# Output projection of a delta-rule attention layer: its first chunks in another order, and o by A of chunks 1 to 3 on VectorE

## What is computed

```
q, k, v = silu(dconv_causal(x @ Wq)), ...        a = sigmoid(x @ Wa + ba)   beta = sigmoid(x @ Wb + bb)
o  = delta_rule(q, k, v, a, beta)                # a scan over 512 tokens, 4 batches, 16 heads of 128 x 128
o  = (o - mean) * rsqrt(var + 1e-5) * ln_w + ln_b    # over the 128 values of each head
o  = o * sigmoid(x @ Wg)
x1 = layernorm(x + o @ Wo)                       # Wo is 2048 x 512
y  = layernorm(x1 + down(silu(x1 @ up) * (x1 @ gate)))   # ternary weights
```

## Time and profile before

| | |
|---|---|
| median of 3 runs | 2786.04 us (2780.75 to 2790.62) |
| the profiled execution | 2770.43 us, its span 2768.7 us |
| TensorE busy in the span | 2549.2 us (92%) |
| VectorE, ScalarE, GpSimd busy | 2039.8, 1164.5, 1439.3 us |
| `attention_out` in the span | about 2013 to 2325 us |

### The profile page before, as it was taken

The page is one execution under the profiler, slowest core; times in us unless marked ns, Lnnn a source line. Parts: engine busy times, 40 slices in busy tenths (PEclk is TensorE's granted clock), DMA queues, the critical chain, the costliest instruction groups (busy, mean ns, idle before and its releaser), DMA issues. The chain is left out here.

```text
span 2768.7 us, 50121 instructions
## 1 busy us (share of the span) xinstructions
PE 2549.2 (92%) x17682; PEld 2205.4 (80%) x17682; DVE 2039.8 (74%) x5887; ACT 1164.5 (42%) x2265; POOL 1439.3 (52%) x1216
## 2 busy tenths in 40 slices
PE   8999999999999589999999999999748897899999
PEld 6888888888888478888898888988637776788887
DVE  4777777677768369999999999999669895333333
ACT  4545444544454222332223322223568784433333
POOL 2644553455346489899998999988322220000000
PEclk9999999999999779999999999999769999999999
DMA  5466546654664765555556656655655544000000
GB/s 134 130 176 172 164 133 176 176 161 135 172 178 140 221 235 213 199 218 200 201 204 236 231 213 234 234 219 199 242 205 197 197 167 153 38 11 11 11 11 15
DMA packets 417317, 454.35 MB, mean 164 GB/s; under 512 B 122496, under 2 KB 367232, under 8 KB 393856
## 3 DMA queue, kind: packets, MB, share of 16 engines
q1 hardware_dynamic: 417152, 452.22, 48.8%
HBM read 321.49 MB, written 131.14 MB: 163 GB/s over the span
## 5 line engine op out<-in xcount | busy, mean ns | idle before, releaser
L355 PE MATMUL pa_ps<-pa_x_hi,pa_w_hi 128*128 128x512 f32 x1296 | 507.8, 392 | 8.2 <-DVE pa_w_lo L394 4.2
L355 PE MATMUL pa_ps<-pa_x_lo,pa_w_hi 128*128 128x512 f32 x1296 | 505.6, 390 | 0.0
L355 PE MATMUL pa_ps<-pa_x_hi,pa_w_lo 128*128 128x512 f32 x1296 | 505.5, 390 | 0.0
L438 DVE SCALAR_TENSOR_TENSOR pa_cv<-pa_y,pa_taps,pa_cv 128x2048 f32<-128x2048 f32 x144 | 359.1, 2494 | 17.8
L1188 DVE TENSOR_TENSOR pb_tmp<-pb_gb,pb_ps 128x112 f32<-128x112 f32 (+6 forms) x1792 | 327.8, 221 | 22.4 <-POOL pb_gb L786 18.1
L1193 DVE TENSOR_TENSOR pb_ps<-pb_ps,pb_tmp 128x112 f32<-128x112 f32 (+6 forms) x1792 | 330.3, 226 | 0.0
L786 POOL TENSOR_TENSOR pb_gb<-pb_gb,pb_ng 128x448 f32<-128x448 f32 (+6 forms) x448 | 319.4, 759 | 7.8 <-DMA pb_gb<-scratch_pairs 4.1
L355 PEld LDWEIGHTS pa_ps<-pa_x_hi,pa_w_hi 128*128 128x128 f32 x1296 | 243.9, 188 | 65.7 <-ACT pa_y L298 8.2
L770 POOL TENSOR_TENSOR all_res<-all_res,pb_crow 128x1024 f32<-128x1024 f32 x120 | 282.4, 2365 | 18.3 <-DMA pb_crow<-scratch_crow 18.3
L355 PEld LDWEIGHTS pa_ps<-pa_x_hi,pa_w_lo 128*128 128x128 f32 x1296 | 244.1, 188 | 51.0
L355 PEld LDWEIGHTS pa_ps<-pa_x_lo,pa_w_hi 128*128 128x128 f32 x1296 | 244.1, 188 | 50.2
(11 more groups left out here) (190 smaller groups left out, 5397.7 us busy)
## 6 DMA issues: line engine op xcount, KB each, us to landing
pb_crow<-scratch_crow SPq DMA_DIRECT2D x30, 2048.0 KB, 10.1
pb_gb<-scratch_pairs SPq DMA_DIRECT2D x64, 896.0 KB, 8.3
pa_o_ng<-scratch_beta SPq DMA_DIRECT2D x16, 1024.0 KB, 7.9
scratch_ng<-pa_o_ng SPq DMA_DIRECT2D x16, 1024.0 KB, 4.5
scratch_A<-pa_o_A SPq DMA_DIRECT2D x16, 1024.0 KB, 4.5
scratch_vt<-pa_o_vt SPq DMA_DIRECT2D x16, 1024.0 KB, 4.5
scratch_q<-pa_o_q SPq DMA_DIRECT2D x16, 1024.0 KB, 6.9
scratch_g<-pa_o_g SPq DMA_DIRECT2D x16, 1024.0 KB, 8.0
```

Source lines behind the costliest of these rows:

```text
L355: last = nc.tensor.matmul(out, w[:, mat, k, :], xx[:, k, b * S:(b + 1) * S], start=(k == 0 and n == 0), stop=(k == KT - 1 and n == 2))
L438: nc.vector.scalar_tensor_tensor(out=out, in0=yy[:, :, k:k + S], scalar=tap(k), in1=out, op0=ALU.mult, op1=ALU.add).then_inc(s_tap, 1)
```

## The change

In the head of `attention_out`:

- o by A of chunks 1, 2 and 3 leaves GpSimd's stream and stands in VectorE's. GpSimd's stream of products begins with chunk 4.
- TensorE does chunk 1's `to_tokens` between blocks 0, 1 and blocks 2, 3 of chunk 0's `to_channels`.
- VectorE sums chunk 1 right behind its half of chunk 0's normalisation; the last eight weight remainders come in one piece behind it; chunk 0's gates are in two halves with chunk 1's normalisation between them.
- ScalarE rounds nine weights first instead of eight, evacuates chunk 0's blocks 2 and 3 only behind chunk 1's squares, and does chunk 1's normalisation before chunk 0's `high`. The squares write into `nrm`, from which chunk 0's blocks are transposed, so there is a new wait for the fourth block.

The regular loops of all engines and SyncE's stream stay as they are. `affine`, `to_channels` and `gate` get an argument `blocks=range(4)`, which is their loop over j.

```diff
 # GpSimd
-            scaled(1, 0, 1)
-            scaled(2, 1, 0)
-            scaled(3, 1, 1)
             with pool.Fori(0, NCH // 2 - 2) as i:
 # ScalarE
-            round_weights(0, 8)
+            round_weights(0, 9)
             squares(0)
             normal(0)
-            round_weights(8, 12)
-            affine(0, 0, True)
+            round_weights(9, 12)
+            affine(0, 0, True, range(0, 2))
             round_weights(12, NH)
+            act.wait_ge(s_b, 4)
+            squares(1)
+            affine(0, 0, True, range(2, 4))
+            normal(1)
             high(0, 0)
-            squares(1)
-            normal(1)
             affine(1, 1, True)
 # TensorE
             to_tokens(0, 0, True)
-            to_channels(0, True)
+            to_channels(0, True, range(0, 2))
             to_tokens(1, 1)
+            to_channels(0, True, range(2, 4))
             pe.wait_ge(s_wo, NH)
 # VectorE
+            def scaled(i, p):
+                dve.wait_ge(s_o[p], 16 * i + 16 * p)
+                dve.wait_ge(s_a[p], 16 * i + 16 * p)
+                nc.vector.tensor_tensor(o_in[p][:, :, :], o_in[p][:, :, :], a_in[p][:, :, :], ALU.mult).then_inc(s_oa, 1)
+
             means(0)
             rest_of_weights(0, 8)
+            scaled(0, 1)
             normal(0, True)
-            rest_of_weights(8, 12)
-            gate(0, 0, 0)
-            rest_of_weights(12, NH)
             means(1)
+            rest_of_weights(8, NH)
+            scaled(1, 0)
+            gate(0, 0, 0, range(0, 2))
+            normal(1)
+            gate(0, 0, 0, range(2, 4))
+            means(2)
             low(0, 0)
-            normal(1)
-            means(2)
+            scaled(1, 1)
             gate(1, 0, 1)
             normal(2)
```

More of the change, by code:

```diff
@@ L1423, in squares, with affine @@
                 nc.scalar.activation(dev[:, :], ssq[:, :], ACT.Sqrt, bias=eps[:, 0:1], scale=1.0 / DV).then_inc(s_dev, 1)
-            def affine(c, p, first=False):
+            def affine(c, p, first=False, blocks=range(4)):
                 if first:
@@ L1429, in affine @@
                     act.wait_ge(s_lo, c - 1)
-                for j in range(4):
+                for j in blocks:
                     act.wait_ge(s_b, 4 * c + j + 1)
@@ L1488, in to_tokens, with to_channels @@
                     last.then_inc(s_t, 1)
-            def to_channels(c, first=False):
-                for j in range(4):
+            def to_channels(c, first=False, blocks=range(4)):
+                for j in blocks:
                     pe.wait_ge(s_na if j < 2 else s_nv, 2 * c + j % 2 + 1)
@@ L1541, in normal, with gate @@
                     last.then_inc(s_nv, 1)
-            def gate(c, i, p):
+            def gate(c, i, p, blocks=range(4)):
                 dve.wait_ge(s_g[p], 16 * i + 16)
-                for j in range(4):
+                for j in blocks:
                     dve.wait_ge(s_ev, 4 * c + j + 1)
```

## The result

The changed kernel took 2767.33 us in the median of 8 runs (2755.23 to 2786.41), the kernel before, run beside it, 2784.86 (2779.88 to 2790.62). The ratio is 0.9934, 95% interval 0.9911 to 0.9956: 18.4 us faster, with 12.3 to 24.8 inside the interval. I had forecast 2775.9 us and 10.1 us of gain, with a range of 2769 to 2784.

What follows compares the result with a forecast made beforehand. The output projection was taken as bound by TensorE's loop behind a late head of ScalarE and VectorE; the first product moves from 2063.2 to 2053.1, a gain of 10.1 us, ratio 0.9964 of 2786.04, so 2775.9 us, range 2769 to 2784.

Steps and rivals of the forecast that it cites:

- What bounds: only the first product's start can be won: Output projection: TensorE paces the loop at 16.7 us a period, so only an earlier first product gains time.
- Start of chunk 0: Head: chunk 1's multiplication takes 2.28 us on VectorE, just hidden; chunk 0's reciprocal starts 1.64 us earlier.
- Chunk 1 between the halves: Head: chunk 1's transposes follow chunk 0's first two blocks; its scalings end at 2035.0 us, before 2048.77.
- the end of 11.8: Head: with chunk 1's 16 transposes at full clock, 1.91 instead of 3.62 us, the gain is up to 11.8 us.
- VectorE is now what ends last: Head: VectorE's remainders, multiplication and gates set the pace; chunk 2's transposes start at 2045.6 us, 11.3 us earlier.
- To the product: Head, chunk 2's transposes to first product: longer than the former 6.28 us; product starts at 2053.1, give or take 0.4.
- The gain: First product starts 10.1 us earlier, kept to the end; sign of being right: 9.5 to 11.5 us earlier.
- How the numbers follow: Whole execution: profiled 2770.43 less 10.1 gives ratio 0.9964; times median 2786.04 gives 2775.9 us, plus range.
- the slow multiplication: Rival, head: multiplication as slow on VectorE as on GpSimd, 4.94 us; gain 5.0, 2781.0 us; chance 0.14.
- the stalls that stay: Rival, head: VectorE's remainders stay slow with GpSimd silent, 1.15 us each; gain 1.6, 2784.4 us; chance 0.02.
- The gain isn't given back: Denies the rival that a late block of chunk 2 or 3 cuts the gain to 0 to 5 us; chance 0.09.
- the loop isn't slower: Denies the rival that GpSimd's multiplication stalls VectorE every loop period: 2.5 us in each of 14, 2811 us; chance 0.05.

Runs made afterwards that it cites:

- the fillers: 8 transposes of the identity matrix ahead of each product's wait, added to the changed kernel; first product to stage end 259.7 to 260.1 us instead of 262.2.
- the two early remainders: Changed kernel with weight remainders 8 and 9 moved ahead of chunk 1's sums on VectorE; head 37.97 us, one execution 2762.4 us.
- before again: The kernel before, unchanged, run against itself: ratio 1.0003, median of 12 runs 2785.4 us.
- loop filled: Changed kernel with 8 transposes of the identity matrix ahead of each product's wait for the og remainder; one execution, 2789.6 us.

## Why the prediction was off

1. *What bounds: only the first product's start can be won.* Right for this change: the loop's periods are the same instructions. But "nothing but" was too strong. The periods aren't all 16.7 us: two to four in each profile take 1.6 us more (two in the profile before), I read only two starts, and the fillers won some 2 us there.
2. *Start of chunk 0.* Right: the multiplication takes 2.28 us and is hidden with 0.38 us to spare, where I had 0.2. Reciprocal 13.03 us behind the stage's first load, as laid out (25.94 - 12.91).
3. *Chunk 1 between the halves.* Mis-sized: I had 22.1 us from the first load to the end of chunk 1's scalings (2035.0 - 2012.91), it took 21.5 (2043.76 - 2022.30), since the clock rose among the transposes. That is the better clock which I had priced as the end of 11.8, for a part of the 16 transposes.
4. *VectorE is now what ends last.* Right, and shown by the two early remainders. Chunk 2's transposes came 31.7 us behind the first load against my 32.7: 0.6 us from step 3, 0.3 from adding up single durations where instructions overlap (eight remainders 4.90 from which the next one starts after 4.81, not 4.96).
5. *To the product.* I had 7.5 us, it took 7.49.
6. *The gain.* 11.1 us in the head in the first pair of profiles, inside my window of 9.5 to 11.5, and 11.6 by the means of both pairs, just outside it; forecast 10.1. The two profiles of the kernel before differ by 0.76 us themselves.
7. *How the numbers follow: "The median of the runs is 2786.04", "with the ratio, 2775.9 us", and a range by "the spread of the runs, which reaches 5.3 below and 4.6 above their median".* This is the step that failed: the terms for the level and for the spread were mis-sized. The three runs, and the five more of the result, happened to lie between 2780 and 2791; 105 lie between 2766.1 and 2804.8 with the median 2780.6, so the level was 5.4 us too high and the spread is 14.5 down and 24.2 up, not 5.3 and 4.6. The profiled execution, 2770.43, lay 10 us below the lowest of the three, and I wrote that down as 0.6% without asking what makes it. From 2780.6, less 10.1, the forecast would be 2770.5 and the range would begin at 2766.1 - 11.8, near 2754. The changed kernel's 20 runs have the median 2767.3. Of the 3.2 us that are left, 1.0 to 1.5 are the head's; the rest is well inside the interval of the medians.

What makes the executions differ was open then. The record settles it, for every execution has its mean granted clock of TensorE beside its time. In 97 executions of the kernel before (the 105 without the eight of the result, which have none on record) this clock lies between 0.952 and 0.970, and the time follows it with a correlation of -0.94: 2.3 us for each 0.001, with a deviation of 3.0 us left of 8.6. The changed kernel's 20 executions give -0.95 and 2.3.

Such a correlation can't say which of the two is the cause. The profiles can, at three places where the same instructions take up to twice the time at the low clock, while TensorE is busy. A long step costs some 6.6 us (70.0 less 63.4); the profiles without one and without a changed recurrence start the stage at 2010.6 to 2019.1 (six of them), the others at 2022.3 to 2045.6. The first chunk takes over 157 us in two profiles (before again and loop filled) and 140 to 148 in the others, and its next step 66.7 there instead of 63.3. In the kernel before, run again, this is the larger part, 14.1 of the 24.8 us by which its stage starts later. TensorE in its profile:

```profile
1066.00:1098.00 32.00, 31.97 (x184) 0.55 0.44 149
```

And a slow period of the loop costs 1.6 us, here with an experiment: with the fillers it doesn't occur.

The same clock accounts for what the runs show beyond the head. Its mean is 0.9670 in the changed kernel's 20 executions and 0.9631 in the 97. As time at the low clock (twice what the mean lacks to 1, times the execution) that is 183 us against 205. 14.5 of these 22 us are the head itself, 50.31 us at 0.56 against 39.22 at 0.62. The other 8 us are worth 3.2 us of execution by an estimate: over the 97 executions, the time grows by 0.41 us with each us at the low clock. With the head's 11.1 to 11.6 this makes 14.3 to 14.8 us, and the means of the runs differ by 13.5. Whether the changed program by itself has less of the low clock ahead of the head isn't shown: the 8 us have a standard error near 6. Not shown either is what in the launch decides where the clock falls.

The rivals: the slow multiplication (2.28 us) and the stalls that stay (4.90 us for eight remainders) are excluded by lines above. The gain isn't given back and the loop isn't slower: from the first product to the end of the stage it is 262.2 us against 262.6. The first product ran at full clock, as the window behind its start shows (1.00).

## What to carry over

Before taking a level from a few runs, lay the profiled execution beside them: if it is outside, find what differs in stages the change doesn't touch, and widen the range by that. Where the mean granted clock of each execution stands beside its time, it says at once whether the clock is what differs. Judge an edit of a few tenths of a per cent by the stretch that it touches in two profiles of each kernel, because whole executions may not resolve it in 20 runs. When work leaves an engine that makes another one stall, price the stalls that go with it by an equal instruction that ran alone.

## What was unexpected

TensorE's clock fell to 1.2 GHz and stayed there for some 13 us while its records leave no idle time, behind 64 matmuls that use 32 rows; 32 matmuls that take 3.68 us at full clock took 6.93 there. The kernel before, run again, has 32 us at a mean of 0.55 with TensorE busy 31.97 of them. The 64 matmuls are no sufficient reason, since every chunk has them. The Trainium skill, TensorE: Matmul & The Clock Gate, "The HAM clock gate", ties the clock to how busy TensorE was; here busy time by the records was not enough to keep it. The same section says that the cold matmuls at a kernel's start vary in number from run to run, and puts the penalty of that ramp below 1% of a typical kernel's span. These falls come in mid-kernel and vary too, and with them one kernel's executions spread over 1.4% (2766.1 to 2804.8 of 2780.6). In the loop, a pause of 1.1 us in a period of 16.7 went with a fall now and then, and 8 transposes in that pause kept the clock up in all four kernels that had them.
